# Four-layer transformer kernel: 24 of 64 indirect row gathers moved ahead into the recurrence, and their sums placed between the gates

## The reference, cut to what matters

```python
def _step(S, inp):                       # inside a scan over time
    q_t, k_t, v_t, g_t, b_t = inp
    S = S * jnp.exp(g_t)[..., None, None]
    v_eff = (v_t - jnp.einsum('bhk,bhkv->bhv', k_t, S)) * b_t[..., None]
    S = S + k_t[..., None] * v_eff[..., None, :]
    o_t = jnp.einsum('bhk,bhkv->bhv', q_t, S)
    return (S, o_t)
...
o = o * jax.lax.rsqrt(jnp.mean(o * o, -1, keepdims=True) + EPS) * norm_w
o = o * g_out * jax.nn.sigmoid(g_out)
return x + o.reshape(B, T, DV) @ Wo
```

```python
slot = jnp.where(mask & (rank <= C), rank - 1, C)
xin = x_pad[idx]                         # the tokens of each expert, packed
h = jax.nn.relu(jnp.einsum('ecd,edh->ech', xin, w1) + b1[:, None, :])
out = jnp.einsum('ech,ehd->ecd', h, w2) + b2[:, None, :]
out = out * jnp.where(valid, tok_w, 0.0)[:, :, None]
final = jnp.zeros((S + 1, d), xf.dtype).at[idx.reshape(-1)].add(out.reshape(-1, d))[:S]
```

## Time and profile before

| | |
|---|---|
| median of three runs | 4294.79 us (4293.73 to 4297.58) |
| the profiled execution | 4300.95 us |
| its span, first to last instruction | 4299.1 us |
| busy share of the span | PE 83%, DVE 58%, ACT 47%, POOL 29% |
| granted TensorE clock, mean | 0.89 |
| recurrence, in the trace | 3188.84 to 3287.39 us |
| out2, in the trace | 3288.36 to 3384.64 us |

### The profile page before, as it was taken

The page is one execution under the profiler, slowest core; times in us unless marked ns, Lnnn a source line. Parts: engine busy times, 40 slices in busy tenths (PEclk is TensorE's granted clock), DMA queues, the critical chain, the costliest instruction groups (busy, mean ns, idle before and its releaser), DMA issues. The chain is left out here.

```text
span 4299.1 us, 87224 instructions
## 1 busy us (share of the span) xinstructions
PE 3566.7 (83%) x28212; PEld 2176.1 (51%) x28212; DVE 2477.0 (58%) x5745; ACT 2010.2 (47%) x3954; POOL 1264.7 (29%) x1810
## 2 busy tenths in 40 slices
PE   5799999849996699963499993768987299999997
PEld 2344444326774222212377772337986166666664
DVE  5577777551114577764677775514846366666664
ACT  5366666513335477761133334323334366566652
POOL 0111111100000011100277771512546444444440
PEclk9799999958997799995799996868869599999999
DMA  4322222100001311100466650111001433333330
GB/s 119 78 56 55 56 55 55 40 0 16 11 6 49 71 43 43 45 18 4 108 158 158 161 131 25 58 58 47 3 3 57 64 117 113 116 115 113 114 112 26
DMA packets 198216, 287.71 MB, mean 67 GB/s; under 512 B 40830, under 2 KB 155204, under 8 KB 197624
## 3 DMA queue, kind: packets, MB, share of 16 engines
q1 hardware_dynamic: 193852, 275.81, 23.1%
q0 software_dynamic: 4096, 8.40, 1.3%
HBM read 232.91 MB, written 35.84 MB: 63 GB/s over the span
## 5 line engine op out<-in xcount | busy, mean ns | idle before, releaser
L692 ACT ACTIVATE att_E<-att_pX,att_gs 128x512 f32<-128x512 f32 (+3 forms) x1024 | 722.4, 740 | 402.1 <-PE att_pX L625 177.7
L725 DVE TENSOR_REDUCE att_mx<-att_pS 128x1 f32<-128x512 f32 (+4 forms) x960 | 730.7, 787 | 279.5 <-PE att_pS L599 179.1
L1831 POOL TENSOR_TENSOR att_E<-att_E,att_rz 128x128 f32<-128x128 f32 (+3 forms) x512 | 357.6, 719 | 436.5 <-DVE att_rz L2039 436.5
L594 PE MATMUL att_pS<-att_ks,att_qs 72*128 72x512 bf16 (+4 forms) x1536 | 410.7, 340 | 59.1 <-DMA att_ks<-parts 34.0
L1541 POOL TENSOR_TENSOR pairs_h<-pairs_m,pairs_r 128x512 f32<-128x512 f32 x272 | 345.5, 1271 | 351.3 <-DVE pairs_m L1604 349.6
L619 PE MATMUL att_pX<-att_qs,att_ks 75*128 75x512 bf16 (+4 forms) x1536 | 422.5, 330 | 30.3 <-ACT att_E L692 15.4
L1565 PEld LDWEIGHTS pairs_po<-pairs_a,pairs_h 128*128 128x128 f32 x2176 | 286.0, 192 | 129.6 <-issue 128.9
L556 POOL CAST att_mp<-att_m 16x128 bf16<-16x128 f32 x288 | 80.5, 279 | 902.6 <-DVE att_m L736 876.9
L636 PE MATMUL att_pO<-att_E,att_vs 128*9 128x512 f32 (+3 forms) x3072 | 322.4, 492 | 1.3 <-ACT att_E L692 1.3
L1586 ACT ACTIVATE pairs_r<-pairs_ph 128x512 f32<-128x512 f32 x272 | 162.4, 597 | 330.5 <-PE pairs_ph L1557 330.5
L1970 ACT ACTIVATE att_E<-att_S,att_nm 128x128 f32<-128x128 f32 (+3 forms) x512 | 282.0, 556 | 38.5 <-DVE att_nm L2033 38.4
(11 more groups left out here) (415 smaller groups left out, 6573.9 us busy)
## 6 DMA issues: line engine op xcount, KB each, us to landing
pairs_c<-weights SPq DMA_DIRECT2D x272, 256.0 KB, 4.0
att_bias<-in_bias_dram SPq DMA_DIRECT2D x64, 896.0 KB, 4.5
parts<-proj_part SPq DMA_DIRECT2D x144, 128.0 KB, 2.3
att_xb<-xnT SPq DMA_DIRECT2D x64, 256.0 KB, 2.7
att_qs<-parts SPq DMA_DIRECT2D x192, 64.0 KB
att_ks<-parts SPq DMA_DIRECT2D x192, 64.0 KB
att_w<-in_w3a_dram SPq DMA_DIRECT2D x64, 192.0 KB, 2.4
att_qs<-parts SPq DMA_DIRECT2D x96, 96.0 KB
```

The source lines that it names most:

```text
L594: ins = nc.tensor.matmul(pS[:, bank, n * w:(n + 1) * w], qs[:K1, u, x, q * P:(q + 1) * P], ks[:K1, u, x, :w], start=(n == 0 or not causal) ...
L692: nc.scalar.activation(E[:, kt % 2, WIDE * xp:WIDE * (xp + 1), :w], places(c)[0], ACT.Exp, scale=gs[:, g % 2, gain_of:gain_of + 1]).then_i ...
L725: V.reduce_max(dst, src, AX.X).then_inc(s_mx, 1)
L1831: nc.gpsimd.tensor_tensor(E[:, k, :width(j)], E[:, k, :width(j)], rz[:, u, k:k + 1].broadcast_to([P, width(j)]), ALU.mult).then_inc(s_n, 1)
```

## The change

The gathers get buffers of their own, `rows`, 16 KB per partition each, that live from the recurrence to the end of out2 in a phase "rows" inside the phase "tiles"; so no gather waits for `inv` and `at`. POOL's list in the recurrence gets one gather behind each of the steps `n` = 0, 1 and 2 of every body: 8 times 3, the gathers `m` = 0 to 23. out2 issues the other 40. `first(0)` and `first(1)` move behind the gates 3 and 5 on ACT, and `second(0)` and `second(1)` behind the sequences 5 and 7 on DVE.

```diff
--- before.py
+++ after.py
@@ -2540,7 +2540,7 @@
                             V.transpose(bc[:, (t + 1) // 2 % 2], brow[:, (t + 1) // 2 % 2]).then_inc(s_bc, 1)
 
 
-def recur_phase(nc, R, name, q, k, kd, inv, at_, last_g, v, own, s_own):
+def recur_phase(nc, R, name, q, k, kd, inv, at_, last_g, v, own, s_own, gather):
 
     with phase(nc, name) as p:
         GW = HALF * HV
@@ -2584,6 +2584,8 @@
                         for m, src in enumerate((k, q, kd)):
                             ins = nc.gpsimd.tensor_tensor(st[:, n, m], both(seqs(src, g, i * 2 + cc)), mine, ALU.mult)
                         ins.then_inc(s_st, 1)
+                        if n < 3:
+                            gather(i * 3 + n)
 
                 for i in range(NBODY):
                     body(i, i == 0, i == NBODY - 1)
@@ -2710,7 +2712,7 @@
                     body(i, i == 0, i == NBODY - 1)
 
 
-def output2_phase(nc, R, name, o, wg, nw, wo, xn, y_all, xr, moe, rows, old):
+def output2_phase(nc, R, name, o, wg, nw, wo, xn, y_all, xr, moe, rows, old, gather, begun, s_get):
 
     SPAN = NC2 * HV // D
     PARTS = HALF
@@ -2730,7 +2732,6 @@
         s_w, s_eps, s_g, s_sg, s_sq, s_ss, s_rt, s_on, s_gt, s_y, s_o, s_a, s_x = (
             p.sem(n) for n in ("w", "eps", "g", "sg", "sq", "ss", "rt", "on", "gt", "y", "o", "a", "x"))
         s_xr = [p.sem(f"xr{n}") for n in range(PARTS)]
-        s_get = [p.sem(f"get{n}") for n in range(PARTS)]
         place = lambda j: j // 2 + j % 2 * HALF
         seq = lambda a, j: a[:, place(j) * T:(place(j) + 1) * T]
         src = lambda j: o[j % 2][:, j // 2 * SPAN:(j // 2 + 1) * SPAN, :].rearrange("p n (c d) -> p (n c) d", d=HV)
@@ -2749,9 +2750,8 @@
 
             @block.gpsimd
             def _(pool):
-                for n in range(NT):
-                    for k in range(2):
-                        nc.gpsimd.indirect_dma_start(rows[k][:, n], None, moe.yout, bass.IndirectOffsetOnAxis(ap=moe.get[:, n, k:k + 1], axis=0)).then_inc(s_get[n // SPAN], 16)
+                for m in range(begun, 2 * NT):
+                    gather(m)
 
             @block.tensor
             def _(pe):
@@ -2807,9 +2807,9 @@
                 root()
                 for j in range(B):
                     gate(j)
-                    if j == 6:
-                        first(0)
-                for q in range(1, PARTS):
+                    if j in (3, 5):
+                        first(j // 2 - 1)
+                for q in range(2, PARTS):
                     first(q)
 
             @block.vector
@@ -2859,10 +2859,10 @@
                     gated(j)
                     if j:
                         result(j - 1)
-                    if j == B - 1:
-                        second(0)
+                    if j in (5, 7):
+                        second(j // 2 - 2)
                 result(B - 1)
-                for q in range(1, PARTS):
+                for q in range(2, PARTS):
                     second(q)
 
 
@@ -3129,8 +3129,6 @@
                 n, j = divmod(m, 2)
                 nc.gpsimd.indirect_dma_start(moe.xin, bass.IndirectOffsetOnAxis(ap=moe.put[:, n, j:j + 1], axis=0), R.s[:, n], None).then_inc(moe.s_put, 16)
 
-        rows = (inv[:, :].rearrange("p (n d) -> p n d", d=D), at_[:, :].rearrange("p (n d) -> p n d", d=D))
-
         conv_phase(nc, R, "conv", (ws, ts, fold), q, k, v, scatter)
         unit_phase(nc, R, "unit", q, k, (to, back, sc))
         with phase(nc, "tiles") as p:
@@ -3146,8 +3144,16 @@
 
             packed_experts_phase(nc, R, "exp2", NE2, CAP2, t["w1_2"], t["b1_2"], t["w2_2"], t["b2r_2"], moe.xin, moe.yout, moe.s_put, 16 * 2 * NT, tiles)
             chunks_phase(nc, R, "chunks", ab, q, k, kd, inv, at_, last_g, cs, bd, own, s_c)
-            recur_phase(nc, R, "recur", q, k, kd, inv, at_, last_g, v, own, s_c)
-        output2_phase(nc, R, "out2", v, t["wg2"], t["nw2"], t["wo2"], park["s"], flat(R.s), k, moe, rows, park["x"])
+            with phase(nc, "rows") as p2:
+                rows = [p2.sb(f"r{j}", [P, NT, D]) for j in range(2)]
+                s_get = [p2.sem(f"get{n}") for n in range(HALF)]
+
+                def gather(m):
+                    n, j = divmod(m, 2)
+                    nc.gpsimd.indirect_dma_start(rows[j][:, n], None, moe.yout, bass.IndirectOffsetOnAxis(ap=moe.get[:, n, j:j + 1], axis=0)).then_inc(s_get[n * HALF // NT], 16)
+
+                recur_phase(nc, R, "recur", q, k, kd, inv, at_, last_g, v, own, s_c, gather)
+                output2_phase(nc, R, "out2", v, t["wg2"], t["nw2"], t["wo2"], park["s"], flat(R.s), k, moe, rows, park["x"], gather, 3 * NC2 // 2, s_get)
 
 
 class Packed:
```

## The result

The changed kernel took 4270.36 us (median of four runs, 4266.54 to 4272.31), the kernel before beside it 4294.6: a ratio of 0.9941, 95% interval 0.9924 to 0.9958. The forecast was 4266, the range 4260 to 4275. The profiled execution took 4268.93 us (span 4267.1, granted clock 0.891).

What follows compares the result with a forecast made beforehand. POOL's 64 gather issues and the last landing were taken to bound out2, the PE-DVE chain the recurrence. Terms -30.1 - 1.0 + 1.1 + 0.7 + 0.5 + 0.2 = -28.6 us gave 4266 us from 4294.79, range 4260 to 4275.

Steps and rivals of the forecast that it cites:

- 24 issues, -30.1: Out2: 24 of 64 gathers leave POOL's train, dropping the issues from 3345.13 to 3375.27, so 30.14 us less.
- Landing, -1.0: End of out2: the last gather's rows land 5.5 us behind its issue instead of 6.54; bounds -1.8 and 0.
- Recurrence, +1.1, +0.7 and +0.5: Recurrence: first gather ahead of step 1's operands +1.1 us, jitter eating POOL's slack +0.7, later clock rise +0.5.
- Changes of phase, +0.2: Around out2: one closing moves behind it and the new phase adds one, 0.2 us more; bounds 0 and 0.5.
- Picks and sums, 0: Out2: the moved first picks on ACT and sums on DVE cost nothing, since gathers still end the phase.
- cover of about 4 us: End of out2: DVE done with part 2 at 3346.7, last rows landing at 3350.6, so gathers still end it.
- A, POOL as the bound: Rival, recurrence: gathers of 1.42 to 1.62 us make POOL the bound, +1 to +5.7 us, 4267 to 4272; chance 0.17.
- B: Rival, tail of out2: DMA engines bound it, a backlog of 5 us would give 4271 us; chance 0.08.
- C: Rival, recurrence: each gather holds DVE's `recur_Sg`, 24 x 0.95 = 23 us on the chain, 4289 us; chance 0.03.
- D: Rival, recurrence: a gather keeps POOL until its rows land when tensor_tensor follows, +80 us, 4345 us; chance 0.02.
- C's own sign: Recurrence: `recur_Sg` taking over 0.9 us would show that a gather holds DVE.

Runs made afterwards that it cites:

- e11: The changed kernel once more, unchanged, beside e9 and e10, where the kernel before took 4297.9 us: 4268.72 us, 0.9933 of the kernel before.
- e10: Changed kernel with ten more gathers begun in POOL's last wait of chunks and DVE waiting later for the weights: 4265.81 us, 0.9925 of the kernel before.
- e12: Changed kernel with ten gathers begun in chunks and DVE's later weights wait, but without the recurrence's first three gathers: 4297.98 us, 0.9945 of the kernel before.
- e8: Changed kernel with the recurrence's gathers behind steps 1 to 3 of each body instead of 0 to 2: 4301.96 us, 0.9954 of the kernel before.
- e2: Changed kernel with the first picks and sums of parts 0 and 1 back in their old places: 4299.77 us, 0.9951 of the kernel before.
- e3: Changed kernel's buffers and new places of the sums, but all 64 gathers in out2: 4322.9 us, 1.0005 of the kernel before.
- e4: Changed kernel with two gathers instead of one behind each of the three steps, 16 left for out2: 4302.18 us, 0.9954 of the kernel before.
- e1: The changed kernel once more, unchanged, where the kernel before took 4323.0 us: 4305.08 us, 0.9957 of the kernel before.
- e7: Changed kernel with each dropped pick's index pointing to a row of its own, not one shared zero row: 4299.31 us, 0.9947 of the kernel before.
- e6: Kernel before with each dropped pick's index pointing to a row of its own, not one shared zero row: 4324.56 us, 1.0008 of the kernel before.
- e9: Changed kernel with out2's 40 gathers paced, eight at once, then fours behind DVE's products: 4273.34 us, 0.994 of the kernel before.

## Why the prediction was right

The total, its range and the mechanism of out2 held. e11, the changed kernel in a later comparison, again on a chip A, took 29.2 us less than the kernel before, the first comparison 24.2; the forecast was 28.6. That the recurrence's part came so near has luck in it, as the terms below show. The forecast took the gathers to end out2, 24 issues to leave it, and the recurrence to take them in for about 2 us. By the terms of the sum, in the two profiled executions of the first comparison:

- **24 issues, -30.1:** first to last gather went from 86.20 us to 56.48, -29.7. The forecast for the 40 was 56.
- **Landing, -1.0:** 3.72 us instead of 6.54, -2.8. That is beyond the bound of -1.8, which I had taken from m=47. e11 has 3.58. The last gathers went out beside DVE's sums, some slower, and so perhaps with less queued ahead of them. No run tested that, and in e10, with fewer gathers, the landing took 8.8 us.
- **Recurrence, +1.1, +0.7 and +0.5:** +1.5 in place of 2.3, by this pair of traces. The gather in front cost 1.45, not 1.1: behind it `recur_Rr` of step 1 comes 6.22 us after the start, and 4.77 (e12) or 4.86 (e8) without it. The clock's rise was put off, as the +0.5 had it. It comes 10.0 us into the recurrence instead of 7.7, and at 10.0 to 11.1 in the seven other runs with a gather behind step 0, against 6.8 to 7.9 in the six without one. The way from step 1 to step 2 became 0.39 us longer. The rest, step 2 to step 30, is 0.34 shorter here, so POOL's lateness, +0.7, shows no cost; it waited 5.8 us in all for `recur_pO` and still had its operands ahead of PE. But one pair of traces can't size so small a sum. In e11, the same kernel, step 30 comes at 96.32, +3.2, 0.9 of it behind step 2, and the kernels with no gather in the recurrence lie between 91.6 and 94.1.
- **Changes of phase, +0.2:** ahead of out2 0.4 less (from DVE's last copy to the first gather), behind it 0.9 more, with two more closings there: +0.5.
- **Picks and sums, 0:** e2 and e3 bear it out on a chip B. The cover of about 4 us that the gathers were to leave DVE was 1.3. ACT still had idle time ahead of gates 4 and 6, 0.4 and 1.4 us.

The terms as measured in this pair make -30.5. The two executions differ by 32.0, of which 2.2 arose ahead of the recurrence and 0.7 went the other way behind out2; neither belongs to the change. The medians differ by 24.2, since the profiled execution of before was 6.4 above its median and that of after 1.4 below.

**The rivals.** A, POOL as the bound, did not come at three gathers a body: behind step 1 PE never waited for `recur_st`. At six (e4) the hand-offs came late before POOL could be the bound, so A stays untested there. B failed, with a landing of 3.72. D failed, with 0.03 us. C was half right: my reading that a gather costs DVE nothing was wrong in the recurrence. `recur_Sg`, two inputs in SBUF, took 0.84 to 0.88 us in the nine steps where it began 0.39 to 0.46 us into a gather with a tensor_tensor behind it; in the three where it began earlier in one it took 0.41 to 0.43. DVE's busy time rose by 6.4 us. C's own sign, over 0.9 us, came too, in three steps (1.10, 1.01 and 2.11), all beside three tensor_tensors of POOL. In out2, with no tensor_tensor behind the gathers, the products kept their 1.41 us, as in the earlier trace rows.

e4 tells which of the two neighbours holds it. There `recur_Sg` began 0.39 to 0.46 us into a gather with a second gather behind it in 11 steps, and took 0.41 to 0.42 in all of them. So the hold goes with the tensor_tensor and not with the gather, though it reaches into the gather's end in the trace; why it does stays open. That is how far the Trainium skill (SBUF — State Buffer, "Who interferes with whom") was nearer: its rule fits the tensor_tensors, which read SBUF, and doesn't come true for the gathers, which read their indices there. I had carried rows of one stage into another in which POOL's next instruction was a different one. In the changed kernel it cost nothing that the trace shows: behind the 1.01 us of step 1 DVE still waited 1.21 us for PE. In e8 it cost the chain 2.0 us.

What the prediction did not know is the other kind of chip. The gains by the medians, 24.2 and 29.2 us on chips A and 18.0 to 23.3 on chips B (e1, e2, e7, e8), differ little against their intervals; the stages tell more. Out2 shrinks by 32.6 us on the first chip and by 28 to 30 on chips B, since its stall is in the kernel before as well. The recurrence grows by 1.5 to 3.2 us on chips A and by 4 to 10 on chips B, where hand-offs in it now come late. The stall at a train of gathers is shown (e1, e4, e12 against e10), and so is that the hot row and the DMA share don't make it (e6). That the engines' updates are held behind those of the gathers is the reading that fits the counts and is not shown: a trace that only fails to record them would count the same, though not make DVE wait; a run that gives the updates pauses on a chip B would test it, and e9 met a chip A. Why chips differ, and why PE's own instructions come 1 to 2 us apart there, stays open.

## What to carry to other kernels

Work that an issuing engine does while all others wait can be worth moving into a stage where that engine has idle time. Here the price was one issue of 1.25 us and a later rise of the clock, both because the first gather stood ahead of operands that were waited for. Before moving it, look at what follows it on its engine: here that set the price for a neighbour. And when a train of small DMAs is on the path, look at more than one chip: what is hidden on one may be a standstill on another.

## What the runs showed of the hardware

- Chips differ here. Beside a train of gathers, one each 1.25 us, hand-offs came late on one kind: 6.1 us from PE to ACT and 15.8 from PE to DVE in e1, both with the train's last landing. On the other kind PE's hand-offs to ACT took 0.04 us in out2 and 0.04 to 0.05 in the recurrence. Stages without gathers differ by up to 4.1 us from one profiled execution to another.
- 128 rows of 512 bytes, gathered each 1.25 us, move at 52 GB/s with a DMA share of 0.88 where many read one row and of 0.19 where each reads its own.
- A gather between two operations of POOL costs 1.25 us at the start of the recurrence (step 1's operand at 2.97 us instead of 1.72), where 0.95 to 1.03 are its own.
- `recur_Sg`, a DVE tensor_tensor with two inputs in SBUF, took 0.41 to 0.42 us beside a gather with a gather behind it (e4, 11 of 11) and 0.84 to 0.88 in the same place with a tensor_tensor behind it (changed kernel, 9 of 9). Beside a row of POOL's tensor_tensors it took up to 2.43 (e8).
- With the first gather ahead of step 1 the granted clock rose from 0.50 to 1.00 10.0 us into the recurrence, with PE busy for 6.02 us of them; without it after 7.7 us, PE busy for 5.21.
